# Last attention: the context tile of the weighting one unit later, in a PSUM bank of its own, and the rows of reciprocals by two transposes

## The reference, cut to what matters

```python
q = ctx_or_rows_normed @ Wq          # here: 1024 query rows per sequence, 16 heads of 64
k, v = split(concat([rows, context]) @ Wkv)   # 1024 token keys and 77 context keys per sequence
sim = einsum('bhid,bhjd->bhij', q * 64 ** -0.5, k)      # masked
attn = softmax(sim, axis=-1)                            # over 1101 keys
out = einsum('bhij,bhjd->bhid', attn, v)
out = layer_norm(einsum('bne,ed->bnd', heads_joined(out), Wout))
```

## Time and profile before

| what | value |
|---|---|
| median of 3 runs (lowest to highest) | 2086.64 us (2085.38 to 2089.72) |
| the profiled execution's own time | 2084.4 us |
| its span, first to last instruction | 2082.6 us |
| mean granted TensorE clock | 0.963 of full |
| stage 6, from its first scores to the start of stage 7 | 1094.0 to 1989.2 us |

### The profile page before, as it was taken

The page is one execution under the profiler, slowest core; times in us unless marked ns, Lnnn a source line. Parts: engine busy times, 40 slices in busy tenths (PEclk is TensorE's granted clock), DMA queues, the critical chain, the costliest instruction groups (busy, mean ns, idle before and its releaser), DMA issues.

```text
span 2082.6 us, 33216 instructions
## 1 busy us (share of the span) xinstructions
PE 1921.5 (92%) x11797; PEld 1355.2 (65%) x11797; DVE 1435.7 (69%) x2676; ACT 978.5 (47%) x2079; POOL 752.3 (36%) x1145
## 2 busy tenths in 40 slices
PE   6997799696999988997878999999999999998999
PEld 3885799542699976883565666666675666655644
DVE  5775111467344457787867999999878999998755
ACT  5672333343111252226875555555545555555455
POOL 1002111000522200000006777777656777777500
PEclk9897899898999999998989999999999999999999
DMA  3702899502489960002002333333222333333201
GB/s 115 208 2 79 273 323 333 170 1 86 163 292 321 310 228 1 1 1 86 1 13 60 82 83 82 83 83 83 72 57 72 82 82 82 82 82 81 63 1 41
DMA packets 191184, 226.87 MB, mean 109 GB/s; under 512 B 28939, under 2 KB 167085, under 8 KB 191021
## 3 DMA queue, kind: packets, MB, share of 16 engines
q1 hardware_dynamic: 183725, 201.98, 33.0%
q0 software_dynamic: 7296, 22.78, 3.3%
HBM read 127.64 MB, written 29.91 MB: 76 GB/s over the span
## 4 chain that ended last, share of the span: by engine, by line
PE 45%; ACT 6%; DVE 3%; issue 1%; POOL 0%; ACTq 0%; DVEq 0%; POOLq 0%
PE ps L640 41%; ACT w_odd L1796 4%; PE ps L1214 2%; PE ps L1215 1%; ACT arena L1785 1%; PE ps L1106 0%; DVE w_odd L2532 0%; DVE small L2410 0%; POOL arena L1908 0%; ACT out_feat L1708 0%; PE ps L1115 0%; ACT xn_tok L1651 0%; DVE small L2522 0%; ACT out_feat L1714 0%; DVE arena L2380 0%
## 5 line engine op out<-in xcount | busy, mean ns | idle before, releaser
L1908 POOL COPY arena<-w_odd 32x512 f32<-32x512 f32 x1024 | 623.7, 609 | 254.4 <-DVE w_odd L2532 202.1
L640 PE MATMUL ps<-arena,w_odd 128*128 128x128 f32 (+4 forms) x2352 | 468.2, 441 | 3.0 <-DVE arena L2202 1.2
L640 PE MATMUL ps<-arena 128*64 128x256 f32 (+4 forms) x3248 | 392.3, 370 | 8.3 <-DVE arena L2333 4.4
L640 PEld LDWEIGHTS ps<-arena 128*64 128x64 f32 (+4 forms) x3248 | 258.9, 155 | 119.5 <-issue 22.6
L2532 DVE STREAM_TRANSPOSE w_odd<-w_odd 128x1024 f32<-128x1024 f32 x256 | 317.4, 1245 | 14.6 <-ACT w_odd L1796 3.0
L1796 ACT ACTIVATE w_odd<-ps,small 128x1101 f32<-128x1101 f32 x256 | 301.6, 1179 | 48.0 <-DVE small L2522 41.0
L640 PEld LDWEIGHTS ps<-arena,w_odd 128*128 128x128 f32 (+3 forms) x2352 | 286.3, 188 | 27.9 <-issue 18.7
L1781 ACT ACTIVATE arena<-ps 77x256 f32<-77x256 f32 x128 | 48.5, 379 | 295.4 <-PE ps L1215 295.4
L2522 DVE TENSOR_REDUCE small<-ps 128x1 f32<-128x1101 f32 x128 | 166.9, 1304 | 29.3 <-PE ps L640 28.1
L1893 POOL DMA_INDIRECT token_rows<-arena x62 | 59.8, 964 | 292.3 <-DVE arena L2223 292.3
L2523 DVE TENSOR_REDUCE small<-ps 128x1 f32<-128x1024 f32 x128 | 155.4, 1214 | 0.0
(11 more groups left out here) (398 smaller groups left out, 2909.8 us busy)
## 6 DMA issues: line engine op xcount, KB each, us to landing
arena<-w_odd SPq DMA_DIRECT2D x1024, 64.0 KB
w_odd<-in_s_w SPq DMA_DIRECT2D x32, 1024.0 KB, 7.4
w_odd<-in_s_wgu SPq DMA_DIRECT2D x30, 704.0 KB, 6.1
w_even<-in_s_w SPq DMA_DIRECT2D x15, 1024.0 KB, 7.3
arena<-expert_rows_in SPq DMA_DIRECT2D x62, 130.0 KB, 4.7
w_odd<-in_s_wd SPq DMA_DIRECT2D x30, 256.0 KB, 3.6
out_feat<-in_s_wgu SPq DMA_DIRECT2D x10, 704.0 KB, 5.9
expert_rows_in<-zero_row POOLq DMA_DIRECT2D x1, 5070.0 KB, 33.2
```

Source lines behind the costliest of these rows:

```text
L640: return pe.matmul(o, lhsT, rhs, start=start, stop=stop, **kw)
L1908: pool.tensor_copy(s6_d[u % 4][32 * j:32 * j + 32, :, 256 * i:256 * i + 256], s6_pm[u % 2][32 * i:32 * i + 32, :, 256 * j:256 * j + 256]). ...
```

## The change

- Weighting: `weigh` is split. `weigh_tokens` (8 token tiles) stays in the odd unit; `weigh_context` (the ninth tile, two matmuls) is issued one unit later, in the even unit, after `sums_turn` and ahead of the pieces. The job "v" is numbered there, and TensorE's signal that the weighting is done comes there.
- Banks: "v" has bank 5 for itself and waits for the multiplication of the group before; all other jobs take banks 6 and 7 in turn and wait for the job two numbers earlier.
- Reciprocals: ScalarE first copies the four columns of reciprocals, each broadcast to 64 columns, into a 128 x 256 block in SBUF (new buffer `s6_rb`, new semaphore `r6_bc`), after its context copy. TensorE then makes two transposes of 128 x 128 from it in place of the four matmuls, and ScalarE copies the result out as before. VectorE's next reciprocal waits for that broadcast copy instead of for TensorE.
- VectorE: the multiplication L2516 moves from the start of the even unit to its end, behind the transposes.
- Output projection, its norm and its addition come one pair of units later (u = 62, 64, 66, 68 and 126, 128, 130, 132).

The diff, with the lines that stand unchanged around the edits cut to those next to them:

```diff
@@ -220,6 +220,7 @@
         s6_r = [cut(AR, 13568 + 256 * i, 2 * P) for i in range(2)]
+        s6_rb = [cut(AR, 14080 + 256 * i, 4, DH) for i in range(2)]
         s6_z = [cut(AR, 14592 + 512 * i, 2, D) for i in range(2)]
@@ -305,6 +306,7 @@
         r6_mm, r6_act, r6_dve = sem("r6_mm"), sem("r6_act"), sem("r6_dve")
+        r6_bc = sem("r6_bc")
         t6_done, copied6, t6_base = t5_c, t5_f, NT
@@ -383,12 +385,12 @@
                 batch += [("r", (u - 2) // 2)]
+            if even and 4 <= u < NU + 4:
+                batch += [("v", (u - 4) // 2)]
             if even and u // 8 < 15:
                 batch += [("w", u // 8 + 1, u % 8), ("w", u // 8 + 1, u % 8 + 1)]
-            if not even and 3 <= u < NU + 3:
-                batch += [("v", (u - 3) // 2)]
-            if even and u >= 4 and (u // 2 - 2) % 32 >= 28:
-                batch += [("o", u // 2 - 2)]
+            if even and u >= 6 and (u // 2 - 3) % 32 >= 28:
+                batch += [("o", u // 2 - 3)]
             if u in N7:
@@ -396,13 +398,14 @@
                 r6_sb[key] = (r6_act if eng == "act" else r6_dve, done[eng])
-        r6_keys = list(r6_no)
+        r6_keys = [key for key in r6_no if key[0] != "v"]
+        r6_turn = {key: i for i, key in enumerate(r6_keys)}
...
-            return 5 + r6_no[key] % 3
+            return 5 if key[0] == "v" else 6 + r6_turn[key] % 2
@@ -1175,9 +1178,11 @@
-                    t = r6_no[key]
-                    if t >= 3:
-                        copied(pe, r6_keys[t - 3])
+                    if key[0] == "v":
+                        if key[1]:
+                            copied(pe, ("v", key[1] - 1))
+                    elif r6_turn[key] >= 2:
+                        copied(pe, r6_keys[r6_turn[key] - 2])
                     return r6_bank(key)
@@ -1216,32 +1221,38 @@
-                    pe.wait_ge(a6_rb, g + 1)
+                    pe.wait_ge(r6_bc, g + 1)
                     bank = free_bank(("r", g))
                     for i in range(2):
-                        for h in range(2):
-                            r = 64 * h
-                            last = mm(PS[r:r + 64, bank, i * P:(i + 1) * P], s6_rc[:, g % 2, 2 * i + h:2 * i + h + 1].broadcast_to([P, DH]), ident[:, :])
+                        last = pe.transpose(PS[:, bank, i * P:(i + 1) * P], s6_rb[g % 2][:, 2 * i:2 * i + 2].rearrange("p a b -> p (a b)"), ident[:, :])
                     last.then_inc(r6_mm, 1)
-                def weigh(g):
+                def weigh_tile(g, i, bank):
                     n = g // 4
+                    s0 = 2 * g % 4
+                    rows = P if i < NKT - 1 else C
+                    for h in range(2):
+                        r = 64 * h
+                        if i < NKT - 1:
+                            p = s6_dw[:, s0:s0 + 2, h].rearrange("p u (q i n) -> p u q i n", q=4, i=8)[:, :, :, i]
+                        else:
+                            p = s6_ptc[g % 2][:, h]
+                        last = mm(PS[r:r + 64, bank, 0:2 * P], s6_v[n % 2][0:rows, i, r:r + 64], p, start=(i == 0), stop=(i == NKT - 1))
+                    return last
+
+                def weigh_tokens(g):
+
                     moved(pe, 2 * g)
                     moved(pe, 2 * g + 1)
+                    bank = free_bank(("v", g))
+                    for i in range(NKT - 1):
+                        weigh_tile(g, i, bank)
+
+                def weigh_context(g):
+
                     copied(pe, ("c", 2 * g + 1))
-                    bank = free_bank(("v", g))
-                    s0 = 2 * g % 4
-                    for i in range(NKT):
-                        rows = P if i < NKT - 1 else C
-                        for h in range(2):
-                            r = 64 * h
-                            if i < NKT - 1:
-                                p = s6_dw[:, s0:s0 + 2, h].rearrange("p u (q i n) -> p u q i n", q=4, i=8)[:, :, :, i]
-                            else:
-                                p = s6_ptc[g % 2][:, h]
-                            last = mm(PS[r:r + 64, bank, 0:2 * P], s6_v[n % 2][0:rows, i, r:r + 64], p, start=(i == 0), stop=(i == NKT - 1))
-                    last.then_inc(r6_mm, 1)
+                    weigh_tile(g, NKT - 1, r6_bank(("v", g))).then_inc(r6_mm, 1)
@@ -1273,13 +1284,15 @@
                         sums_turn((u - 2) // 2)
+                    if even and 4 <= u < NU + 4:
+                        weigh_context((u - 4) // 2)
                     if even and n < 16:
...
                     if not even and 3 <= u < NU + 3:
-                        weigh((u - 3) // 2)
-                    if even and u >= 4 and (u // 2 - 2) % 32 >= 28:
-                        project(u // 2 - 2)
+                        weigh_tokens((u - 3) // 2)
+                    if even and u >= 6 and (u // 2 - 3) % 32 >= 28:
+                        project(u // 2 - 3)
                     if u in N7:
@@ -1781,6 +1794,12 @@
                         g = (u - 2) // 2
+                        act.wait_ge(a6_rb, g + 1)
+                        if g >= 2:
+                            act.wait_ge(r6_mm, r6_no["r", g - 2] + 1)
+                        act.activation(s6_rb[g % 2], s6_rc[:, g % 2].unsqueeze(2).broadcast_to([P, 4, DH]), ACT.Copy).then_inc(r6_bc, 1)
+                    if even and 2 <= u < NU + 2:
+                        g = (u - 2) // 2
                         bank = filled(("r", g))
@@ -1798,8 +1817,8 @@
                             piece(n, i, filled(("w", n, i))).then_inc(r6_act, 1)
-                    if even and u >= 4 and (u // 2 - 2) % 32 >= 28:
-                        g = u // 2 - 2
+                    if even and u >= 6 and (u // 2 - 3) % 32 >= 28:
+                        g = u // 2 - 3
                         t = 8 * (g // 32) + 2 * (g % 4)
@@ -2507,13 +2526,6 @@
                     even = u % 2 == 0
-                    if even and 4 <= u < NU + 4:
-                        g = (u - 4) // 2
-                        c = (g // 4) % 8
-                        q0 = 2 * P * (g % 4)
-                        bank = filled(("v", g))
-                        copied(dve, ("r", g))
-                        dve.tensor_tensor(s6_ot[c][:, q0:q0 + 2 * P], PS[:, bank, 0:2 * P], s6_r[g % 2], ALU.mult).then_inc(r6_dve, 1)
                     if u < NU:
@@ -2533,14 +2545,21 @@
                             if g >= 2:
-                                dve.wait_ge(r6_mm, r6_no["r", g - 2] + 1)
+                                dve.wait_ge(r6_bc, g - 1)
                             dve.reciprocal(s6_rc[:, g % 2], s6_sm[:, g % 2]).then_inc(a6_rb, 1)
-                    if even and u >= 6 and 28 <= (u // 2 - 3) % 32 < 31:
-                        added(u // 2 - 3)
-                    if even and u >= 4 and (u // 2 - 2) % 32 >= 28:
-                        normed(u // 2 - 2)
-                    if not even and u >= 5 and ((u - 1) // 2 - 2) % 32 == 31:
-                        added((u - 1) // 2 - 2)
+                    if even and 4 <= u < NU + 4:
+                        g = (u - 4) // 2
+                        c = (g // 4) % 8
+                        q0 = 2 * P * (g % 4)
+                        bank = filled(("v", g))
+                        copied(dve, ("r", g))
+                        dve.tensor_tensor(s6_ot[c][:, q0:q0 + 2 * P], PS[:, bank, 0:2 * P], s6_r[g % 2], ALU.mult).then_inc(r6_dve, 1)
+                    if even and u >= 8 and 28 <= (u // 2 - 4) % 32 < 31:
+                        added(u // 2 - 4)
+                    if even and u >= 6 and (u // 2 - 3) % 32 >= 28:
+                        normed(u // 2 - 3)
+                    if not even and u >= 7 and ((u - 1) // 2 - 3) % 32 == 31:
+                        added((u - 1) // 2 - 3)
                     if u == 72:
```

## The result

The changed kernel takes 2138.15 us (median of 4 runs, 2137.79 to 2141.95) against 2086.01 of the kernel before on the same chips: ratio 1.0251, 95% interval 1.0233 to 1.0269. It is 52 us slower. The prediction was 2135.6 us, in a range of 2114 to 2156.

What follows compares the result with a forecast made beforehand. TensorE was taken as the bound in odd units, with 0 to 0.3 us of slack in even ones. Even units +60, odd -17, end +6 gave +49 on 2084.4; plus 2.2 for the median, 2135.6 us, range 2114 to 2156.

Steps and rivals of the forecast that it cites:

- The tile out of the odd unit: Odd units: TensorE loses the tile's 0.45 us, so the unit falls from 6.55 to the exponentials' loop at 6.24: -0.31.
- The new wait: Even units: TensorE stands 0.90 us (0.76 to 1.07) for ScalarE's broadcast copy, which is queued behind the context copy.
- Reciprocals and tile on TensorE: Even units: two transposes take 0.38 us instead of 0.58 for four matmuls (-0.20); the tile adds 0.45.
- Units: Scores to scores, even units: 7.1, 7.5, 7.5, 7.2 us for j = 0, 2, 4, 6; +60 even, -17 odd.
- The exponentials: Even units: the first exponential starts at S + 4.28 instead of 3.68, making the loop 6.84 us; matters only without pieces.
- Banks: Waits for banks cost zero, except up to 0.6 us in two units where a projection waits for the first piece's copy.
- The end of the stage: Units 120 to 126 and three projections instead of two behind unit 127: +6 us together.
- The sum: Whole program: +49 us on the profiled execution's 2084.4, then 2.2 for the median: 2135.6; own case 2121 to 2153.
- A: Rival: the broadcast copy is ready by S + 2.52, so TensorE never stands; 2081.6 us, faster; chance 0.03.
- B: Rival: odd units give nothing, the next scores still starting at 6.55, so the -17 us is gone; 2153 us; chance 0.06.
- C: Rival: the new pauses make the clock fall; 2160 us if each fourth pair, 2229 if each pair; chance 0.07.
- D: Rival: the broadcast copy runs largely inside the context copy's time, TensorE stands 0.5 us; 2112 us; chance 0.06.

Runs made afterwards that it cites:

- Copy first: The changed kernel with ScalarE's broadcast copy issued ahead of its context copy; ratio to the kernel before 1.0006, 2088.3 us.
- copy twice: The changed kernel with a second copy of the same kind and size ahead of the broadcast copy; ratio to the kernel before 1.0344.
- tile in the pause: The changed kernel with the context tile issued ahead of the reciprocals' transposes on TensorE, ScalarE's order unchanged; ratio to the kernel before 1.0080.
- transposes only: The kernel before with only the reciprocals changed: broadcast copy behind the context copy, two transposes; ratio to the kernel before 1.0125.
- banks only: The kernel before with only the banks changed: bank 5 for the weighting, two in turn for the rest; ratio to the kernel before 1.0011.
- the four transposes in a row: The kernel before with broadcast copy ahead of context copy, two reciprocal transposes, and both units' context turns together in the even unit; ratio 0.9901, 2068.5 us.
- transposes first: The kernel before with only the reciprocals changed to two transposes, and the broadcast copy ahead of the context copy; ratio 0.9981, 2083.5 us.
- tile only: The changed kernel with the reciprocals spread by four matmuls as before, no broadcast copy or transposes; ratio to the kernel before 1.0033.

## Why the prediction was right, point by point

- **The tile out of the odd unit**, -0.31: 6.24 measured, as worked out. j = 7 is 6.33, although its exponentials start at S + 3.68 and S + 4.92 as in the others. The code has two more waits ahead of the scores of the next head pair (for its pieces 6 and 7); that they are the 0.09 is not shown.
- **The new wait**, 0.90 of standing, 0.76 to 1.07 as ends: transposes at S + 3.35 instead of 2.52, 0.83, with a pause of 0.77 in the row, 64 times, 50.1 us. The copy took 0.40 (0.42 taken) and started 0.28 after the context copy, not 0.38. Copy first, copy twice and tile in the pause show that this is the cause: the pause was taken away, lengthened by 0.31 and filled with work, and each time the length of the units followed.
- **Reciprocals and tile on TensorE**, 0.38 + 0.45 = 0.83: 0.37 + 0.58 = 0.95 in their place. The tile was sized wrong, as 4 of 36 records. Standing between full-width jobs it adds 0.67 (0.95 against 0.28 in transposes only): see the last section. The transposes were taken 0.10 too dear, so two misses cancel in part. Together reciprocals and tile take 0.12 more than predicted and the wait 0.07 less, so pieces start at S + 4.30 where 4.25 was predicted.
- **Units**: 7.10 / 7.51 / 7.49 / 7.17 predicted for even j, 7.09 / 7.56 / 7.55 / 7.15 measured. Units 0 to 119: +60 in even and -17 in odd units predicted, +60.3 and -16.8 measured. So this sum holds in both of its parts.
- **The exponentials**: S + 4.28 predicted, S + 4.11 measured, again because copies overlap. Units without pieces take 6.59, not 6.84.
- **The multiplication**, zero: in the odd unit the mask starts at 1435.31, 1.43 after the scores, as before.
- **Banks**, zero and up to 0.6 in two units: 0.5 to 1.1 in four, 3.3 us (banks only). The mechanism was named; its size and the number of units were too small.
- **The end of the stage**, +6: 8.9. The miss lies behind unit 127: +7.2 predicted, 38.0 us instead of 27.3 measured, +10.7. There the granted clock fell to 0.50 (from 2015.19 to 2020.19). TensorE had paused 0.73 and 1.34 us there, and the first 8 projection records, 2.00 us in the earlier trace rows, lasted 3.78:

```profile
2013.89 0.69 PE L1227 MATMUL ps<-ident,arena 128*128 128x128 f32 x2 [1.34 <-ACT arena L1800]
...
2015.56 3.78 PE L643 MATMUL ps<-w_even,xn_tok 128*128 128x256 f32 x8
```

  That these pauses made it fall was not tried. The run tile in the pause speaks for it: its two pauses there are 0.34 and 0.76, its clock stays at 1.00, and its end takes 86.9 instead of 92.0.
- **The sum**: 2135.6 predicted, 2138.15 measured, and part of this closeness is luck. The sum was +49 on a profiled execution, and +54 was measured there: 0.6 of the difference in units 0 to 119, 2.9 in the end, 1.6 ahead of the stage. I then added 2.2 because the median before lay that much above its profiled execution; the median after lies 0.2 below its own. The upper end of my own case is also added wrongly: +10 + 6 + 3 gives 2155, not 2153.
- **Rivals.** A (the copy hides) is the run copy first: it came out at 1.0006 and not faster. Its middle gained 6.0 us, where A had 7 - 17 = -10: the even units outside 60 to 70 cost 6.6 and the odd ones gave 15.6, but units 60 to 70, with the projections that wait for a bank, cost 2.9. Its end grew by 5.8. B (the odd units give nothing) fell with 6.24 there. D (the stall is half) fell with 0.83, not 0.5. C (the clock) fell: pauses of 0.77 in each pair left the granted clock at 1.00 from 1125 to 1900 us, units 4 to 111:

```profile
1125.00:1900.00 775.00, 724.30 (x4562) 440.85 (x4556) 650.12 (x939) 409.13 (x816) 530.60 (x872) 1.00 0.31 75
```

## What to carry to other kernels

An operand that is moved to another engine brings that engine's queue with it: read what stands ahead of the new instruction in its order, and whether that waits for the very engine that will wait. Here 0.4 us of copying, put one place too late, made a ring TensorE, ScalarE, TensorE and cost 2.4% with the tile beside it, 1.4% without; put ahead, into idle time that the trace showed as 2.99 us, it cost nothing. And when an engine and a loop are within 0.3 us of each other, moving work between units pays only as far as the loop; taking work away in both kinds of unit (the four transposes in a row) brought what moving it did not.

## What the runs showed of the hardware that was not expected

The price of a small TensorE job depended on its neighbours. All times here run from the start of one job to the start of the next.

- Transposes in a row start 0.10 to 0.17 us apart (four from context turn to reciprocals in 0.50). Two of them took 0.38 where 64-column matmuls followed, 0.22 where full-width matmuls did (transposes first), and 0.28 there behind a pause (transposes only).
- The four matmuls of the reciprocals, 64 columns wide, took 0.58 ahead of full-width pieces and 0.49 ahead of the tile (tile only).
- The tile added 0.44 behind those matmuls. Behind full-width transposes it added 0.67: from transposes to pieces 0.89 instead of 0.22 (copy first against transposes first), and 0.95 instead of 0.28 (the kernel after against transposes only).

Each change between 64-column and full-width work thus cost about 0.1 to 0.16 us here. That the change of shape is the reason was read from the rows of six kernels, and not tried on its own.
